# Filler products, an earlier start of attention and a freer order in a fused transformer block

## The reference

```python
x = x + layernorm(attention(layernorm(x)))
x = x + layernorm(moe(layernorm(x)))
# attention: 32 query heads, 8 key/value heads (4 query heads share one), head size 16,
#            rotary embedding on q and k, causal softmax over 1024 keys, output projection
# moe: softmax router over 64 experts, top 6, capacity 128 rows for each expert,
#      gated experts (512 -> 2 x 192 -> 512), plus a shared gated expert (512 -> 2 x 384 -> 512)
```

## Time and profile before

| | us |
|---|---|
| median of 3 runs | 2303.48 (2288.59 to 2321.18) |
| profiled execution | 2303.76 |
| its span, first to last instruction | 2301.7 |
| PE busy | 1964.9 (85%) |
| DVE busy | 1314.6 (57%) |
| ACT busy | 1042.5 (45%) |
| POOL busy | 718.4 (31%) |
| mean granted TensorE clock | 0.921 |

### The profile page before, as it was taken

How to read it: one execution, slowest core, us unless ns; L and a number is a source line. 1 busy time by engine, 2 the same in 40 slices (tenths; PEclk the granted TensorE clock), 3 DMA queues, 4 the chain that set the end, 5 groups by cost and what they waited for, 6 DMA issues and landing times.

```text
span 2301.7 us, 41702 instructions
## 1 busy us (share of the span) xinstructions
PE 1964.9 (85%) x12707; PEld 976.5 (42%) x12707; DVE 1314.6 (57%) x2831; ACT 1042.5 (45%) x1568; POOL 718.4 (31%) x985
## 2 busy tenths in 40 slices
PE   6999979989999799889997979899979688998930
PEld 3434335544333355543343545334345344444410
DVE  4588836546798265468982654688736312222248
ACT  2557753334677433446774334567733222222200
POOL 2212214522222145222222452122215422222248
PEclk9889989987899899979998999799989899999975
DMA  2122323310000121100001110000002199999988
GB/s 84 55 93 94 127 87 111 137 54 2 11 16 12 33 98 67 38 6 11 12 12 42 62 59 21 6 12 12 16 28 75 62 300 322 335 335 315 339 252 293
DMA packets 108130, 232.81 MB, mean 101 GB/s; under 512 B 24423, under 2 KB 24423, under 8 KB 107920
## 3 DMA queue, kind: packets, MB, share of 16 engines
q1 hardware_dynamic: 81072, 191.07, 23.9%
q0 software_dynamic: 24576, 35.07, 6.3%
q10 hardware_dynamic: 2272, 4.06, 0.5%
HBM read 141.59 MB, written 126.48 MB: 116 GB/s over the span
## 4 chain that ended last, share of the span: by engine, by line
PE 59%; DVE 12%; issue 10%; DMA 7%; ACT 3%; POOL 2%; DVEq 2%; SPq 1%; another core or an unknown queue 1%; POOLq 1%; ACTq 0%
PE ps L759 9%; DVE rmax L1212 8%; PE ps L698 7%; PE ps L653 6%; DMA gx<-dispatch_scratch 6%; PE ps L898 5%; PE ps L845 4%; PE ps L779 4%; PE ps L871 3%; PE ps L930 3%; PE ps L884 3%; PE ps L654 3%; PE ps L673 2%; PE ps L872 2%; PE ps L705 2%
## 5 line engine op out<-in xcount | busy, mean ns | idle before, releaser
L1212 DVE TENSOR_REDUCE rmax<-ps 128x1 f32<-128x512 f32 (+3 forms) x1280 | 732.5, 632 | 188.0 <-PE ps L708 114.2
L1038 ACT ACTIVATE pr<-ps 128x1024 f32<-128x1024 f32 (+3 forms) x768 | 586.2, 813 | 239.4 <-PE ps L779 233.2
L698 PE MATMUL ps<-kT,qT 48*128 48x512 f16 (+3 forms) x1536 | 396.5, 349 | 34.0 <-DVE rmax L1212 23.8
L759 PE MATMUL ps<-pr,v_ones 128*32 128x512 f32 (+3 forms) x3072 | 348.1, 528 | 7.9 <-POOL pr L1488 4.5
L1488 POOL TENSOR_SCALAR_AFFINE_SELECT pr<-pr 128x512 f32<-128x512 f32 x256 | 162.2, 638 | 502.5 <-ACT pr L1038 501.1
L779 PE MATMUL ps<-qT,kT 50*128 50x512 f16 (+3 forms) x1536 | 301.4, 344 | 17.0 <-ACT pr L1038 7.9
L698 PEld LDWEIGHTS ps<-kT,qT 48*128 48x128 f16 x1536 | 123.3, 95 | 343.8 <-DVE rmax L1212 282.8
L1534 POOL DMA_INDIRECT dispatch_scratch<-x,slot_i x192 | 190.1, 990 | 73.4 <-issue 73.4
L705 PE MATMUL ps<-above,sel 64*128 64x128 bf16 x1024 | 190.1, 227 | 0.0
L898 PE MATMUL ps<-gu_sb,gxT 128*128 128x384 f32 x512 | 189.0, 493 | 0.0
L1553 POOL DMA_INDIRECT acc_scratch<-eo,etok x64 | 98.7, 1541 | 282.5 <-DVE eo L1351 270.3
(11 more groups left out here) (149 smaller groups left out, 2599.0 us busy)
## 6 DMA issues: line engine op xcount, KB each, us to landing
gu_sb<-w_gu_dram SPq DMA_DIRECT2D x64, 768.0 KB, 7.6
dn_sb<-w_dn_dram SPq DMA_DIRECT2D x64, 384.0 KB, 9.0
dispatch_scratch<-blank SPq DMA_DIRECT2D x8, 2308.0 KB, 8.8
gx<-dispatch_scratch SPq DMA_DIRECT2D x64, 288.5 KB, 5.2
xin<-x_dram SPq DMA_DIRECT2D x32, 256.0 KB
acc_scratch<-blank SPq DMA_DIRECT2D x32, 256.0 KB, 2.1
xres<-x_dram SPq DMA_DIRECT2D x32, 256.0 KB
x_scratch<-x SPq DMA_DIRECT2D x32, 256.0 KB, 2.0
```

What stands on the lines that cost most here:

```text
L698: last = pe.matmul(o, qT[r:r + SROWS, half, 2 * g + h // 2, q % QPH * P:(q % QPH + 1) * P], kT[r:r + SROWS, g, kh * HALF:kh * HALF + w], s ...
L759: last = pe.matmul(ps[32 * h:32 * h + 32, 6, c0:HALF], v_ones[g % 2][:, kt, :], pr[i % SLOTS][:, h, 0:HALF - c0], start=kt == 0, stop=kt = ...
L1038: act.activation(pr[i % SLOTS][:, 2 * pair:2 * pair + 2, 0:HALF - c0], ps[:, 2 + 2 * pair:4 + 2 * pair, 0:HALF - c0], ACT.Exp, scale=facto ...
L1212: dve.tensor_reduce(dst[:, heads[0] % 2, heads[0] // 2:heads[0] // 2 + n, q % QPH], ps[:, BANK_OF[item], 0:n * w].rearrange("p (h k) -> p ...
```

## The change

- `plan_attention` now puts **products of ones** (128x128 by 128x512, bf16, into a bank that is about to be overwritten) ahead of S^T and of ring units. It sums the modelled PE work of the last `SPAN` us, each kind with a weight (products with v 1.0, S^T 0.78, stacks 0.7, scores 0.37), and adds up to four products until the sum reaches `ENOUGH` times `SPAN`. Phase 1 gets 20 of them ahead of its first wait for `x2_ready` and 10 ahead of the last wait for `hid_ready`.
- The preparation has **eight steps**. Stacks of tile s-1 are made in step s: the first ahead of the last 256-column product, the other two behind the next `x_transpose`. Tile 6's stacks join tile 7's in the planned order. Early units have five slots in a step from step 2 on: 21 of them, and `t0` of group 0 in step 6, one step and more earlier.
- ACT's and POOL's work on tile 7 (`highs`, `lows`) and the copy of v are in the planned order too. ACT waits for tile 7's `lows` only at tile 2 of group 0, since `pr2` and `pr3` now lie where the wait matters. The first product with v no longer waits for all stacks.
- The `t0` and `t1` transposes are a **queue of their own** and take whichever bank is free first, as do ring units and tile 7's stacks. S^T ranks ahead of ring units.

```diff
+FIRST_FILL = 20
+LAST_FILL = 10
...
 def early_plan():
...
+    for step in range(2, TT):
+        ready = [("u", 0, u) for u in range(NU) if UNITS[u][1] == step - 2]
+        for slot in range(-1, DC):
+            if slot == 0:
+                queue += ready
+            if step == TT - 2 and slot == -1:
+                plan.append((step, slot, ("t0", 0)))
+            elif queue:
+                plan.append((step, slot, queue.pop(0)))
...
+    SPAN, ENOUGH, FILL, MOST = 3.42, 0.43, 0.214, 4
...
+    turnq = [("t1", 0)] + [(part, g) for g in range(1, KVH) for part in ("t0", "t1")]
...
+    def next_bank():
+        return min(BANKS, key=lambda bank: (bank_free(bank), BANKS.index(bank)))
...
+    def fillers(at):
+        lo = at - SPAN
+        done = sum(part * max(0.0, min(end, at) - max(start, lo)) for start, end, part in runs[-40:])
+        return min(MOST, max(0, math.ceil((ENOUGH * SPAN - done) / FILL)))
...
-                choices.append((at, 2, "one"))
+            choices.append((max(at, can_score(item)), 3, "one"))
...
-            choices.append((at, 3, "st"))
+            choices.append((at, 2, "st"))
...
-        pr = [sb(f"pr{k}", [P, REP, HALF], f32, wa) for k in range(SLOTS)]
+        pr = {k: sb(f"pr{k}", [P, REP, HALF], f32, wa) for k in (2, 3, 0, 1)}
...
+                def keep_warm(bank, n):
+
+                    for _ in range(n):
+                        pe.matmul(ps[:, bank, :], ones_b[:], ones_b[:].unsqueeze(1).broadcast_to((P, HALF // P, P)),
+                                  start=True, stop=True)
...
                     for item in items:
                         free_bank(item)
                         if item[0] == "u" and item[1] == 0:
                             pe.wait_ge(stack_copied, 3 * (TT * b + UNITS[item[2]][1] + 1))
+                    keep_warm(BANK_OF[items[0]], fill)
...
-                for s in range(TT + 1):
-                    early = [item for step, item in EARLY if step == s]
-                    for c in range(DC):
-                        if s < TT:
-                            qkv_chunk(s, c)
-                        if s >= 2 and c < 3:
-                            stack_transpose(s - 2, c)
-                        if early and (c >= 1 or s == TT):
-                            ring([early.pop(0)])
+                for s in range(TT):
+                    early(s, -1)
+                    for c in range(DC - 1):
+                        qkv_wide(s, c)
+                        qkv_rest(s, c)
+                        early(s, c)
+                    qkv_wide(s, DC - 1)
+                    early(s, DC - 1)
+                    if 1 <= s < TT - 1:
+                        stack_transpose(s - 1, 0)
+                    qkv_rest(s, DC - 1)
                     if s + 1 < TT:
                         x_transpose(s + 1)
-                    for item in early:
-                        ring([item])
+                    if 1 <= s < TT - 1:
+                        stack_transpose(s - 1, 1)
+                        stack_transpose(s - 1, 2)
...
-                        if g == 0:
-                            pe.wait_ge(stack_copied, 3 * TT * (b + 1))
...
+                        if t == 0:
+                            keep_warm(7, FIRST_FILL)
                         pe.wait_ge(x2_ready, n + 1)
...
+                        if t == TT - 1:
+                            keep_warm(2, LAST_FILL)
+                        pe.wait_ge(hid_ready, n + 1)
...
-                for s in range(TT + 1):
-                    if 1 <= s and s + 1 < TT:
-                        normalise(b, s + 1)
-                    if 1 <= s <= TT:
+                for s in range(TT):
+                    if s >= 1:
                         rotate(s - 1)
...
+                rotate(TT - 1)
                 for item in STREAM:
```

More of the change, by code:

```diff
@@ L141, in act_choices @@
         out = []
-        for j, at in turned.items():
-            if j not in stacked:
-                out.append((max(now["act"], at + LAT), 0, ("stack", j)))
+        for tj, at in turned.items():
+            if tj not in stacked:
+                out.append((max(now["act"], at + LAT), 0, ("stack",) + tj))
+        if not high:
+            out.append((max(now["act"], rotated + LAT), 0, ("high",)))
         if expq and expq[0] in st:
@@ L216, in bank_free, with reduce_next, on_act @@
-    def bank_free(item):
-        occupant = held[BANK_OF[item]]
+        if high and TT - 1 not in lows:
+            out.append((max(now["pool"], high[TT - 1] + LAT), 0, ("low",)))
+        return out
+    def reduce_next():
+        item = redq.pop(0)
+        w, heads = UNITS[item[2]][3:]
+        now["dve"] = red[item] = max(now["dve"], scored[item] + LAT) + 0.065 + len(heads) * w / 960
+        if item[2] == NU - 1:
+            now["dve"] = red[item] = now["dve"] + 0.3
+    def on_act(at, what):
+        act.append(what)
+        if what[0] == "exp":
+            expq.pop(0)
+            now["act"] = ex[what[1:]] = at + 0.172 + 2 * (HALF - PUNITS[what[2]][2]) / 1200
+        elif what[0] == "raw":
+            rawq.pop(0)
+            now["act"] = copied[what[1:]] = at + 0.6
+        elif what[0] == "stack":
+            now["act"] = stacked[what[1:]] = at + 1.02
+        elif what[0] == "high":
+            now["act"] = high[TT - 1] = at + 1.7
+        else:
+            now["act"] = freed[what[1]] = at + 0.27
+            rows[what[1]] = now["act"] + ROWS
@@ new lines, in follow, with bank_free @@
+    def follow(until):
+        while True:
+            while redq and redq[0] in scored:
+                reduce_next()
+            steps = [(c, on_act) for c in act_choices()] + [(c, on_pool) for c in pool_choices()]
+            if not steps:
+                return False
+            (at, _, what), do = min(steps, key=lambda step: step[0][:2])
+            if at > until:
+                return False
+            do(at, what)
+            if until < FAR:
+                return True
+    def bank_free(bank):
+        occupant = held[bank]
@@ L229, in plan_attention @@
+    while stq or pvq or ring or stackq or turnq:
+        while redq and redq[0] in scored:
+            reduce_next()
         choices = []
         if stackq:
[L231 to L232 removed]
+            t, j = stackq[0]
+            at = lows.get(t, FAR) + LAT
+            if t == TT - 1:
+                at = max(at, bank_free(next_bank()))
+            elif j == 2:
+                at = max(at, stacked.get((t, 0), FAR) + LAT)
             choices.append((max(now["pe"], at), 0, "stack"))
```

285 lines of the change are left out of this document (141 added, 144 removed).

## The result

The changed kernel is **slower**: 2387.93 us, median of 4 runs (2375.34 to 2411.99), against 2312.33 us of the kernel before on the same chip (4 runs, 2288.59 to 2344.51). The ratio is 1.0407, 95% interval [1.0275, 1.0538]. Forecast were 2238 us and a range of 2205 to 2290. The profiled execution took 2375.89 us with a span of 2373.8: 72.1 us more than the span before. (Medians are of all runs; ratios leave disturbed runs out, and an experiment given without a ratio had a single run left, too few for one.)

What follows compares the result with a forecast made beforehand. PE at half clock was taken to bound the 30.5 us in which attention begins. Terms 42.8 - 8 + 8 + 9 + 3 + 8 + 4.4 = 67.2 us off 2303.8 gave 2236.6, rounded to 2238; range 2205 to 2290.

Steps and rivals of the forecast that it cites:

- period stays 25.5 to 26 us: Sign of being right: steady attention groups keep this period, with L698's wait for DVE unchanged.
- that rival: Steady groups: S^T first delays ring units and starves DVE, 3.06 us in each of 28 groups, 86 us lost; chance 0.08.
- some 9 us: Hand-over of row maxima through POOL, ACT, SP and DMA, said to set group 0's second half; in a rival of chance 0.08.
- when POOL is idle: no cost: Preparation: `finish_half` takes about 1 us of POOL's time ahead of `highs`; no cost, 1 us a batch without that cover.
- The start: Start of attention: at DVE's pace 10.7 us a batch go, 42.8 in four; 20 products cost 2 a batch, half hidden.
- the first rival: Start of attention: clock falls all the same, too few products where stacks count for less; gain 37 us, 2266; chance 0.20.
- Five units and earlier stacks in the preparation: Preparation: five more early units gain 2 us a batch, stacks one step after their tile net 2.2.
- Phase 1: Products of ones ahead of tile 0 gain 8 us in all, those at the end 4.4 us.
- 4.4 forecast: End of phase 1: ten products of ones shorten L884, 2.4 + 0.3, 1.7 and 0 us, nothing in batch 3.
- 3.7 as a sign of being right: Start of phase 1: L845 of tile 0 takes 3.7 us, where it had taken 4.36.
- Dips: Group 1 of batches 1 and 2: the clock's further fall goes away, 1.5 us each, 3 us.

Runs made afterwards that it cites:

- e4: Kernel before with one edit, ring units ranked behind S^T, no products of ones, banks in turn: 2410.03 us.
- e1: Changed kernel with S^T ranked behind ring units again, ring and row-max transposes held to S^T's pace: 2332.39 us, ratio 1.0123.
- e2: Changed kernel with only the planner's figure for the hand-over of row maxima, `ROWS`, set from 2.1 to 4.7 us: 2324.97 us, ratio 1.0202.
- e3: Changed kernel in exactly its order with all products of ones left out, in attention and phase 1: 2375.18 us, ratio 1.0414.
- e5: Changed kernel with group 0's `t0` transpose and its ACT copy moved from step 6 to step 7: 2364.85 us, ratio 1.0377.
- e16: Changed kernel's preparation and early tile 7, later `t0`, the kernel before's order from group 1 on, products of ones in phase 1 only: 2330.11 us.
- e15: Kernel before in its order, with 28 products of ones a batch in attention by the change's rule, each made twice: 2349.26 us, ratio 1.0343.
- e17: As e16 but without any product of ones, against the kernel before: 2313.25 us, ratio 0.9965.

## Why the prediction was wrong

- **The failed step: that the steady groups' "period stays 25.5 to 26 us" with S^T ranked first.** I priced the rank only as delay to ring units (14 of 24 pairs, 2.4 us a group, 0.08). The loss has that size, 88 us against 86 in that rival, but the match is luck: in groups 1 to 6 the rank acts by another mechanism. S^T first shortens the time from `t1` to the S^T that needs it below the hand-over of 6.4 us, PE stands still, and the clock falls behind it. I named this hand-over ("some 9 us") for group 0 only, and never held it against the 23 items that covered it in the other groups. Shown by e4 (the rank alone brings it), e1 and e2 (the waits of groups 1 to 6 are gone without the rank, and with the true `ROWS`) and e3 (not the products). The fewer items stand between, the longer the wait: 1.4 to 2.1 us behind 8 or 9, 2.4 to 3.0 behind 4, 4.3 behind one (e5).
- **What late maxima don't explain.** e1 and e2 leave some 30 us of the 88 each. In e2 17.9 of them are the last group's. There, with S^T first, 7 ring units are left over that the kernel before had done by then, and DVE reduces for 4.1 us in it (0.2 before); with the rank undone (e1) the group takes 22.8 us. How the 17.3 us divide between this and the wait for the maxima was not measured. What e1 leaves lies in the order of groups 1 to 6 and is all but gone in e16 (5 us in all batches together); which part of the order costs it stays open.
- **`finish_half` "when POOL is idle: no cost".** POOL was idle, and then stood still for 4.1 us that no edit made: 5.9 us for each of three batches, shown by e5. The row with 4.10 us of idling was in the trace of before; I had looked at how busy POOL is, not at how soon it answers. I gave 1 us as the price without cover.
- **The start: -10.7 us a batch, less 2 for products.** It gave -5.9. Half clock stayed for 13.7 to 20.5 us, so the first rival (clock falls all the same) was half true. The worth of the clock was sized about right: 9.1 us for 27.3 us of it, by e15, against 10.7 for 30.5. What failed is that products do this freely. I took half of them as hidden; by my estimate from e15 all were on the path. And most of the gain needs none: the new order alone, tile 7 earlier, cuts half clock to 17 to 20 us and the start to 44 to 47 us (e3, e17). The Trainium skill ("TensorE: Matmul & The Clock Gate", part 4) says that transposes don't count as busy in the same way for the clock; that half clock stayed for 13.7 us or more under the planner's 0.7 for stacks is in line with it, but no run here changed that weight alone.
- **Five units and earlier stacks in the preparation: +2 and +2.2 a batch.** Without the POOL stall the preparation is 69.6 us (e5) against 68.8: nothing gained, 0.8 lost. The gain of units moved shows in the start instead, inside its 5.9 us; the two can't be told apart by these runs.
- **Phase 1: +3.1 us a batch.** Measured 3.0 in the profiled pair and 2.2 as a mean over more of them, but only where ACT's odd wait of 8 us is there; nothing otherwise. The sum agrees partly by luck: the end gave its 4.1 us in the first three batches (4.4 forecast), the 20 products at the start 0.4 us a batch instead of 2.0, and L845 of tile 0 (now L917) stayed over 4 us where I had named 3.7 as a sign of being right.
- **Dips: +3 us.** The other way: 119.5 us more of half clock in groups 1 to 6, a consequence of the waits: in e2, which has none of them there, half clock is gone from these groups.
- **Slips in the working.** PE's 4.3 us of idling ahead of L653 are 3.6 us for the copies of xT and 0.7 us of issue, and three chunks and a half at 1.29 us are 4.5 us, not 4.7. Neither changes a term by more than 1 us a batch.

Added up: +88 (groups) +20.7 (preparation) -23.8 (start) -11.9 (phase 1) -0.7 (rest) = 72.3 us, the span's difference of 72.1.

## What to carry to other kernels

Before a rank in a list scheduler is changed, list each hand-over that crosses engines and measure it end to end in the trace; compare it with the work that the order keeps between its two ends, not with the planner's own constant. Where PE's order is fixed ahead, one late operand stops everything behind it, and here a second price of the same size followed in the clock. Look at the last group by itself: it has less work to cover a hand-over than the steady ones. In a stretch that PE bounds, each product of ones cost its full time here, about as much as the clock gave back; even where PE stood still anyway, ahead of phase 1's tile 0, 20 of them brought 0.4 us.

## What the runs showed of the hardware

- Four DMAs of one small tile from one queue land 4.2 us after their source is ready; 2.4 us of it is the issue of the first three.
- POOL needs 4.1 us between two plain instructions the first time that it comes to them in batches 1 to 3, never in batch 0. The profile names no releaser, and the cause is open.
- With 40 extra products of 512 columns in the start of attention, the same instructions ran at half clock for 3.4 us in one batch and for 20.5 in another (e15); the longer one took 5.7 us more. Behind a single wait of 1.4 to 2.1 us for a maximum the clock is at half for nothing to 10.2 us (after), and in e1's fourth group it is at half for 13.7 us in batches 1 to 3 and not at all in batch 0, where PE waited as long.
- ACT waits 6.6 to 8.8 us once a batch, in every batch of nine of the profiles and in none of the other eleven, for something that the profile calls remote.
